# Output matmuls of the second attention one batch ahead, normalization on ScalarE, expert steps spread over four iterations

## What is computed

```python
x = x + attn_a(layernorm(x))                      # 16 heads of 8, rotary, causal
x = x + ffn(layernorm(x), expert_sel, keys, values)
x = x + attn_b(layernorm(x), WQ, WK, WV)          # 1 head of 128, banded scores
x = x + ffn(layernorm(x), expert_sel, keys, values)

# attn_b: scores outside a band of 64 are multiplied by 0, then softmax over all 512
score = einsum('bqd,bkd->bqk', q, k) / sqrt(128) * band
y = einsum('bqk,bkd->bqd', softmax(score), v)

# ffn: 64 experts, the best 4 of each token
sel = sigmoid(x @ expert_sel.T);  val, idx = top_k(sel, 4)
y = sum over the 4: (relu(x @ keys[idx]) * val) @ values[idx]
```

## Time and profile before

| | us |
|---|---|
| three timed runs | 1121.22 median, 1119.34 to 1125.25 |
| the profiled execution | 1114.41 |
| its span, first to last instruction | 1112.7 |
| busy: PE, DVE, ACT, POOL | 800.1, 741.7, 566.7, 727.1 |

### The profile page before, as it was taken

How to read it: one execution, slowest core, us unless ns; L and a number is a source line. 1 busy time by engine, 2 the same in 40 slices (tenths; PEclk the granted TensorE clock), 3 DMA queues, 4 the chain that set the end, 5 groups by cost and what they waited for, 6 DMA issues and landing times.

```text
span 1112.7 us, 22610 instructions
## 1 busy us (share of the span) xinstructions
PE 800.1 (72%) x7290; PEld 584.2 (53%) x7290; DVE 741.7 (67%) x2033; ACT 566.7 (51%) x1513; POOL 727.1 (65%) x860
## 2 busy tenths in 40 slices
PE   1789988788878877679779766655556899898000
PEld 0444443444434432579779765444445888898000
DVE  3687898888878842576465666888979575576111
ACT  1167767675757665456536444444344556465000
POOL 6245748887875758665666462477777656666776
PEclk8689999998989988889979888776667999899555
DMA  6456645543237223359868651011113778898322
GB/s 192 135 197 209 211 164 197 175 137 100 84 94 236 61 70 101 107 161 270 237 172 245 174 141 37 29 50 52 50 52 103 216 215 240 233 270 250 93 61 64
DMA packets 206547, 163.82 MB, mean 147 GB/s; under 512 B 15968, under 2 KB 191072, under 8 KB 206432
## 3 DMA queue, kind: packets, MB, share of 16 engines
q1 hardware_dynamic: 183968, 110.43, 34.4%
q0 software_dynamic: 16384, 33.59, 10.2%
q10 hardware_dynamic: 6080, 18.35, 4.4%
HBM read 78.94 MB, written 83.36 MB: 146 GB/s over the span
## 4 chain that ended last, share of the span: by engine, by line
PE 36%; POOL 19%; DVE 17%; issue 12%; DMA 9%; ACT 6%; POOLq 0%; ACTq 0%; SPq 0%; DVEq 0%
PE ps L789 7%; PE ps L798 6%; POOL sorted_rows L1736 5%; PE ps L690 5%; DMA x_scaled<-result_rows,dest 3%; PE ps L778 3%; PE ps L649 3%; POOL y_heads L1750 2%; ACT arena L1001 2%; POOL arena L1782 2%; DVE row_max L1236 2%; POOL x_scaled L1750 2%; POOL xn L1757 2%; PE ps L698 1%; DVE block_max L1236 1%
## 5 line engine op out<-in xcount | busy, mean ns | idle before, releaser
L1001 ACT ACTIVATE arena<-ps 128x512 f32<-128x512 f32 x320 | 183.0, 598 | 74.5 <-PE ps L622 73.2
L1736 POOL DMA_INDIRECT sorted_rows<-v_aug,dest x128 | 128.4, 1003 | 86.6 <-DVE dest L1423 36.1
L1736 POOL DMA_INDIRECT sorted_rows<-x_scaled,dest x128 | 126.4, 987 | 43.1 <-issue 28.0
L789 PE MATMUL ps<-arena 128*128 128x128 f32 x1024 | 144.9, 287 | 10.3 <-DVE arena L1435 8.9
L1435 DVE COPY arena<-ps 128x512 f32<-128x512 f32 x128 | 88.3, 690 | 94.2 <-PE ps L778 93.7
L649 PE MATMUL ps<-arena 64*128 64x128 bf16 (+3 forms) x576 | 129.0, 302 | 28.5 <-DMA arena<-k_parts 15.1
L1236 DVE TENSOR_REDUCE row_max<-ps 128x1 f32<-128x512 f32 (+1 forms) x192 | 126.9, 681 | 30.7 <-PE ps L669 29.5
L990 ACT COPY arena<-ps 128x512 f32<-128x512 f32 x128 | 74.9, 585 | 137.1 <-PE ps L798 136.9
L798 PE MATMUL ps<-arena 128*128 x1024 | 139.4, 281 | 0.9 <-ACT arena L990 0.9
L789 PEld LDWEIGHTS ps<-arena 128*128 128x128 f32 x1024 | 132.7, 202 | 13.3 <-DVE arena L1435 9.9
L622 PE MATMUL ps<-arena 64*128 64x512 bf16 (+3 forms) x512 | 124.4, 311 | 16.2 <-ACT arena L1001 13.5
(11 more groups left out here) (221 smaller groups left out, 1648.8 us busy)
## 6 DMA issues: line engine op xcount, KB each, us to landing
arena<-sorted_rows SPq DMA_DIRECT2D x128, 256.0 KB
result_rows<-arena SPq DMA_DIRECT2D x128, 256.0 KB
sorted_rows<-arena ACTq DMA_DIRECT2D x16, 1024.0 KB, 5.0
arena<-q_parts SPq DMA_DIRECT2D x16, 512.0 KB, 4.0
arena<-k_parts SPq DMA_DIRECT2D x16, 512.0 KB, 5.0
q_parts<-parts SPq DMA_DIRECT2D x52, 128.0 KB, 2.9
k_parts<-parts SPq DMA_DIRECT2D x38, 128.0 KB, 3.0
sorted_rows<-x_scaled,dest POOLq DMA_INDIRECT x128
```

The source lines that it names most:

```text
L789: mm = pe.matmul(ps[:, e_bank(2, layer, half, n), P * i:P * i + P], ktile[:, v, P * i:P * i + P], xtt[:, v, P * i:P * i + P], start=True, ...
L1001: nc.scalar.activation(prob[:, grp % 2, pr % 2, PROB_AT[u]:PROB_AT[u] + T], ps[:, v % 2, :], ACT.Exp, scale=SCALE_A).then_inc(exp_done, 1)
L1736: g.indirect_dma_start(sorted_d[b // HALF][:, :], bass.IndirectOffsetOnAxis(dest[:, 16 * b + n:16 * b + n + 1], 0), scaled_rows(layer, b)[ ...
```

## The change

- `BJOBS`: P01, P23, O move to offset 1, and the order of jobs within an iteration becomes S01, S23, RK, VO, P01, P23, O, NT, LG, XT, Q, K, V, TB on PE. O has bank 5 to itself; V now shares bank 1 with S01, P23 and LG.
- `BESIDE`: the half (0, 1) takes 14, 11, 5 and 4 steps in iterations -2 to 1; the half (1, 0) begins at place 5 of iteration 7 (9 steps).
- The norms are applied by ACT (`apply_norm`, jobs N3 and N2, ahead of NT), as Identity with a per-token scale and bias; DVE computes the bias with one instruction more (`negb`, semaphore `shifts`).
- ACT runs VO, `scale` (first and second half), E, P01, P23, N3, N2, NT, LG and the projections in this order. DVE runs `outside_sums` behind place 0 and the positions behind place 4.

```diff
@@ -87,14 +87,15 @@
 
 
 
-BJOBS = [(7, "P01", 0), (1, "P23", 0), (5, "O", 0), (1, "S01", 1), (3, "S23", 1), (1, "RK", -1), (5, "NT", 0), (6, "LG", 0),
-         (3, "XT", 2), (6, "Q", 2), (7, "K", 2), (3, "V", 2), (5, "VO", 1), (6, "TB", -1)]
+BJOBS = [(1, "S01", 1), (3, "S23", 1), (6, "RK", -1), (7, "VO", 1), (7, "P01", 1), (1, "P23", 1), (5, "O", 1), (3, "NT", 0),
+         (1, "LG", 0), (7, "XT", 2), (3, "Q", 2), (7, "K", 2), (1, "V", 2), (6, "TB", -1)]
 FIRST_IT_B, LAST_IT_B = -2, B + 1
 WIN = 192
 OUTSIDE = T - WIN
 PLACES = 14
-BESIDE = {(0, 1): {-2: (3,) + 13 * (1,), -1: PLACES * (1,), 0: (1, 0, 0, 1, 0, 0, 1, 0, 0, 1, 0, 0, 0, 0)},
-          (1, 0): {7: 6 * (0,) + 8 * (1,), 8: PLACES * (1,)}}
+BESIDE = {(0, 1): {-2: (2,) + 12 * (1,) + (0,), -1: (0, 1, 1, 0) + 9 * (1,) + (0,), 0: (0, 1, 0, 1, 0, 1, 0, 1, 0, 1, 0, 0, 0, 0),
+                   1: (0, 1, 0, 1, 0, 1, 0, 1, 0, 0, 0, 0, 0, 0)},
+          (1, 0): {7: 5 * (0,) + 9 * (1,), 8: PLACES * (1,)}}
 
 
 def steps_beside(it, place):
...
@@ -900,29 +903,28 @@
 
             apart(0, expert_step)
             for it in range(FIRST_IT_B, LAST_IT_B + 1):
+                attend(it, "S01", "S23")
+                beside(it, 0)
+                attend(it, "RK", "VO")
+                beside(it, 1)
+                beside(it, 2)
                 attend(it, "P01")
-                beside(it, 0)
+                beside(it, 3)
                 attend(it, "P23")
-                beside(it, 1)
+                beside(it, 4)
                 attend(it, "O")
-                beside(it, 2)
-                attend(it, "S01", "S23")
-                beside(it, 3)
-                attend(it, "RK")
-                beside(it, 4)
                 beside(it, 5)
+                beside(it, 6)
                 attend(it, "NT")
-                beside(it, 6)
+                beside(it, 7)
                 attend(it, "LG")
-                beside(it, 7)
+                beside(it, 8)
                 attend(it, "XT")
-                beside(it, 8)
+                beside(it, 9)
                 attend(it, "Q", "K")
-                beside(it, 9)
+                beside(it, 10)
+                beside(it, 11)
                 attend(it, "V")
-                beside(it, 10)
-                attend(it, "VO")
-                beside(it, 11)
                 beside(it, 12)
                 attend(it, "TB")
                 beside(it, 13)
...
@@ -1088,7 +1090,22 @@
                 act.wait_ge(bank_ready[bank], n + 1)
                 return ps[:, bank, :], bank_free[bank]
 
+            def apply_norm(i, b, dst, done):
+
+                for t in range(TT):
+                    nc.scalar.activation(dst[:, t, :], x[:, TT * b + t, :], ACT.Identity, bias=negb[:, i, t:t + 1],
+                                         scale=rsb[:, i, t:t + 1]).then_inc(done, 1)
+
             def attention_b(name, b):
+                if name == "N3":
+                    act.wait_ge(shifts, b + 3)
+                    act.wait_ge(scaled, 16 * (B + b - 1))
+                    apply_norm(1, b, xn1[:, b % 2], norm3)
+                    return
+                if name == "N2":
+                    act.wait_ge(shifts, b + 1)
+                    apply_norm(0, b, xn0, norm2)
+                    return
                 if name == "E":
                     act.wait_ge(nrow_done, b + 1)
                     nc.scalar.activation(probw[:, b % 2, :, WIN], nrow[:, b % 2, :], ACT.Exp)
...
@@ -1130,7 +1147,7 @@
                     expert_step(*step)
 
             def attend(it, *names):
-                offs = {name: off for _, name, off in BJOBS} | {"E": 1}
+                offs = {name: off for _, name, off in BJOBS} | {"N2": 2, "E": 1}
                 for name in names:
                     b = it + offs.get(name, 0)
                     if 0 <= b < B:
...
@@ -1139,35 +1156,34 @@
             apart(0, expert_step)
             act.wait_ge(band_made, BANDS)
             for it in range(FIRST_IT_B, LAST_IT_B + 1):
-                attend(it, "P01")
                 beside(it, 0)
-                attend(it, "P23")
-                beside(it, 1)
+                attend(it, "VO")
                 r = it - 1
                 if 0 <= r < B:
                     act.wait_ge(top_seq, 12 * (B + r) + 12)
                     act.wait_ge(norm3, TT * r + TT)
                     scale(1, r, range(0, 8))
-                beside(it, 2)
-                beside(it, 3)
-                attend(it, "E")
+                beside(it, 1)
                 if 0 <= r < B:
                     scale(1, r, range(8, 16))
-                beside(it, 4)
-                beside(it, 5)
-                attend(it, "NT")
-                beside(it, 6)
+                beside(it, 2)
+                attend(it, "E", "P01")
+                beside(it, 3)
+                attend(it, "P23")
+                for place in (4, 5, 6):
+                    beside(it, place)
+                attend(it, "N3", "N2", "NT")
+                beside(it, 7)
                 attend(it, "LG")
-                beside(it, 7)
+                beside(it, 8)
                 attend(it, "XT")
-                beside(it, 8)
+                beside(it, 9)
                 attend(it, "Q", "K")
-                beside(it, 9)
+                beside(it, 10)
+                beside(it, 11)
                 attend(it, "V")
-                beside(it, 10)
-                attend(it, "VO")
-                for place in (11, 12, 13):
-                    beside(it, place)
+                beside(it, 12)
+                beside(it, 13)
             apart(1, expert_step)
             for s in range(STEPS):
                 expert_step(1, 1, s)
...
@@ -1211,12 +1227,8 @@
                     nc.vector.scalar_tensor_tensor(out=rs if last else y, in0=half, scalar=1.5, in1=y,
                                                    op0=ALU.add, op1=ALU.mult).then_inc(rstd_b if last else root_seq, 1)
                 dve.wait_ge(rstd_b, n + 1)
-
-            def apply_norm(i, b, dst, done):
-
-                for t in range(TT):
-                    nc.vector.tensor_scalar(dst[:, t, :], x[:, TT * b + t, :], mvb[:, i, t, 0:1], rsb[:, i, t:t + 1],
-                                            ALU.subtract, ALU.mult).then_inc(done, 1)
+                nc.vector.scalar_tensor_tensor(out=negb[:, lo:hi, :], in0=mvb[:, lo:hi, :, 0], scalar=-1.0, in1=rs,
+                                               op0=ALU.mult, op1=ALU.mult).then_inc(shifts, 1)
 
             def maxima(pr, u):
                 p = pr % 4
...
@@ -1625,6 +1637,8 @@
                 if route:
                     finish(choose(B + r, *evacuated("LG", r)))
                 beside(b, 0)
+                if 0 <= b + 1 < B:
+                    outside_sums(b + 1)
                 beside(b, 1)
                 if attend:
                     score_out(b)
...
@@ -1639,22 +1653,12 @@
                     combined_stats(far)
                 if attend or prepare:
                     inverse_roots(0 if prepare else 1, 2 if attend else 1)
-                if attend:
-                    dve.wait_ge(scaled, 16 * (B + b - 1))
-                    apply_norm(1, b, xn1[:, b % 2], norm3)
-                if prepare:
-                    if far:
-                        bank, n = bjob["XT", far - 1]
-                        dve.wait_ge(bank_ready[bank], n + 1)
-                    apply_norm(0, far, xn0, norm2)
                 beside(b, 4)
-                if 0 <= b + 1 < B:
-                    outside_sums(b + 1)
-                beside(b, 5)
                 if route:
                     bank, n = bjob["RK", r]
                     place_rows = positions(B + r, ps[:, bank, :], bank_ready[bank], n + 1, bank_free[bank], n + 1)
                     advance(place_rows, 6)
+                beside(b, 5)
                 beside(b, 6)
                 if route:
                     finish(place_rows)
```

More of the change, by code:

```diff
@@ L266, in build @@
         rsb = sb("rs_b", [P, 2, TT])
+        negb = sb("neg_mean_rs_b", [P, 2, TT])
         guess = sb("root_guess", [P, 2, TT])
@@ L405, in build @@
         rstd_b = sem("rstd_b")
+        shifts = sem("shifts_b")
         norm2 = sem("norm2")
```

## The result

| | before | after |
|---|---|---|
| median of 20 runs each, us | 1118.28 (1112.73 to 1127.92) | 1127.35 (1121.70 to 1133.65) |
| ratio, 95% interval | | 1.0081 (1.0061 to 1.0101) |
| the profiled execution, its span | 1114.41, 1112.7 | 1133.65, 1131.7 |

A forecast was written before the change was run, and what follows sets the result against it. The prediction took POOL, issuing indirect DMAs, as the bound, with two waits for DVE's destinations. Its terms -0.8 + 4.9 + 2.2 gave +6.3 us, on 1121.2 a forecast of 1127.5 us, range 1114 to 1137.

The forecast's parts named there:

- stage 4: Step 0 of the second layer's first half to the eighth destinations: one expert step more, +2.2 us (1 to 4).
- stage 5: After the eighth destinations: scatter and gathers follow without a wait for results, 0 within 2 us.
- Stage 1: Up to the first scatter of the second expert layer: -0.8 us, bounds -6 to +7.
- Stage 2: From the second layer's first scatter to scale's end in iteration 5, paced by POOL's unchanged order: 0 us.
- Stage 3: From scale's end in iteration 5 to step 0 of the second layer's first half: +4.9 us (2.4 to 7).
- (a): Scale's end to choose of batch 5: E, P, O and norms now between; 9.7 us, not 4.8, so +4.9.
- (b): The turn from choose of batch 5 to that of batch 6: 24.5 to 26.5 us against 24.6, +0.9.
- (c): Choose of batch 6 to step 0: DVE loses four norms and gains a small product, -0.9 us.
- The weighed rule: The skill's VectorE for adds and multiplies: iteration 5's norms on DVE would make the whole sum +3.9 us.
- The clock stays full: Rival: PE's idle times get shorter with P, O and steps spread; -1 us, 1120 us; chance 0.25.
- Every lone step at half clock: Rival: expert steps standing singly among waits all run at half clock; +18 us, 1139 us; chance 0.12.
- POOL bounds all the way: Rival: the wait before the eighth scatter goes; -6 to -11 us, 1110 to 1116 us; chance 0.18.

The follow-up runs named there:

- batches 1 to 3: The changed kernel with ACT's scale multiplications of batches 1 to 3 alone moved behind V: 1125.02 us, ratio 1.0055 to the kernel before.
- scale late: The kernel before, with its scale multiplications of batches 1 to 5 moved behind V: 1143.83 us, ratio 1.0226 to the kernel before.
- scale of batches 4 and 5 late: The changed kernel with scale of batches 4 and 5 moved behind V: 1112.90 us, ratio 0.9946; with the norms also back on DVE 1117.83 us.

## Why the prediction was right, and where its terms were off

The time (1127.5 against 1127.35) is nearer than its terms deserve. The forecast added 6.3 us to a base of 1121.2, the median of three runs; twenty runs have it at 1118.28. The change costs 9.1 (6.8 to 11.3 by the interval): the base was 2.9 too high and the sum 2.8 too low. By stages, in the two profiles (stage 4 from the starts of its first and last rows, 51.12 to 50.76 us, stage 5 to the end of the span):

| stage | predicted | measured |
|---|---|---|
| 1, up to X | -0.8 | -2.3 |
| 2, X to Z | 0 | +2.3 |
| 3, Z to step 0 | +4.9 | +8.5 |
| 4, step 0 to the eighth scatter | +2.2 | -0.4 |
| 5, the rest | 0 | +2.4 |

**Stage 1** is right within its bounds, but not by its sum. As listed, the terms of iteration -1 add up to 38.9 us, not 39.6, and those of iteration 1 to 37.3, not 35.5: X at 706.4, so +0.3 instead of -0.8, and +7.4 in all. The spread table of (0, 1) is worth nothing: with the old table the stage took 147.9. What moved it is the norms, as far as single profiles tell: with them on DVE it took 150.8 in both runs, with them on ACT 145.7 to 148.9.

**Stage 2**, the pacing by POOL, was the premise, and batches 1 to 3 show it: choose of batch 4 came 16.5 us earlier against X than after (75.7 for 92.2), choose of batch 5 only 1.2. It holds only while something that choose needs stands behind scale in iteration 5, and the prediction took that for the kernel's nature, where it is a choice of order. By its rule "an edit pays only if it moves X, the 41.4 or the 50.8" it didn't look for an edit that makes Z harmless. That was worth 14 us. The +2.3 shows in POOL's own pace, with no wait for DVE in it: its fourth scatter begins 105.6 us behind X before (106.2 with scale late), 107.8 after, and 106.6 to 109.5 in the other runs. What slows it stays open.

**Stage 3**, the mechanism, is right: E, P, O and the norms between scale and NT's copy, and POOL's wait grown (12 predicted, 14.8 measured). Its size was short by 3.6. (a) Choose stood 11.6 us behind Z, not 9.7. The sum let O's 2.0 us run beside the norms' 3.3. The norms did take 3.19, but O at half clock took 3.7 and was the later of the two, and NT's four transposes (1.06) come behind it; the sum had them only in the turn. (b) The turn was 27.1, not 25.5: O alone makes 1.5 of the difference (3.7 against 2.2). (c) 11.2 against 11.0. The price of a norm on ACT (0.41) was right, 3.19 / 8 = 0.40, but not on the path: NT waits for O. Two of the prediction's signs were just missed: X came at 712.16, 0.16 behind its window, in a profile that was 8.4 us late from the start, and step 0 stood 49.9 us behind Z, not 44 to 49.

**The weighed rule.** By the sum without ACT's norms I had +3.9 instead of +6.3. The run with norms on DVE isn't faster than the change (1.0102 against 1.0081, overlapping intervals), and with scale of batches 4 and 5 late they cost 4 to 5 us on DVE. The Trainium skill, "ScalarE: Activation LUTs", section "Rules for kernel authors", prefers VectorE for adds and multiplies. Eight norms are indeed shorter there (2.14 against 3.19 us), but the kernel with them on DVE isn't the faster one; the measurement decides otherwise here, since DVE's own work bounds the turn of iteration 5 once scale is late.

**Stage 4** was right by cancellation only. The step costs 3.3 to 3.6 us (2.2 predicted, within 1 to 4); the stage behind choose became 3 us shorter, which the prediction didn't see.

**Rivals.** "The clock stays full" is refuted by the 0.50 from P to LG, and filling PE, which kept the clock full in iterations 2, 3 and 6, gave 1124, not 1120; in iteration 5, behind the paced scale, O still ran at half clock, so the rival's own condition wasn't met there. "Every lone step at half clock" didn't happen (mean clock 0.88 and 0.93 in stages 1 and 4). "POOL bounds all the way" needed stages 3 and 4 under 87.5 us; they took 100.7.

What stays open: why stage 4 behind choose is 3 us shorter, and stage 5's +2.4; over all runs of the changed code that stage took 205.8 to 210.2, and the kernel before has 207.2, so it may be no effect of the change.

## What to carry to other kernels

On an in-order engine, a step that waits for a slow queue should not stand ahead of the chain that feeds that queue's next work; look where each engine idles after the reorder, and put the work with slack there. A saving ahead of a paced step vanishes in its wait, and so does every other remedy there, so test the paced step first. When one work item is pulled ahead an iteration, all its neighbours' places on the other engines have to be chosen again.

## What the runs showed of the hardware

PE's clock answered to the idle gaps inside one iteration, and it cost more than I had allowed. The timelines of PE at P of iteration 2, in the kernel after and in the one with TensorE filled:

```profile
729.96 1.96 PE L883 MATMUL ps<-ident,y_heads 128*128 128x128 f32 x8 [6.53 <-ACT y_heads L1114]
```

```profile
726.41 1.04 PE L887 MATMUL ps<-ident,y_heads 128*128 128x128 f32 x8
```

With 6.53 us of idle time ahead of P in iteration 2 of the kernel after it was granted 0.50 (1.2 GHz) from P to LG; with that gap filled by matmuls whose results nobody reads it stayed at 1.00, and the turn was 5 us shorter, as much as by moving scale. The Trainium skill, "TensorE: Matmul & The Clock Gate", section "What's actually happening", says that the throttled state is the default and activity releases the throttle; the trace agrees.

At half clock P, O and LG took 1.8 to 1.9 times as long as at full clock (1.96 to 1.04, 3.7 to 2.0, 1.94 to 1.08 us).
